# An attention and gated feed-forward layer on one core: the last group's scores two heads abreast

## The chip, the cores and the metric

The kernel runs on one core of a Trainium2 chip. The time is device microseconds of the whole program, the median of several runs. One further execution was taken by the profiler; its span is the time from its first to its last recorded work.

## What is computed

```python
xn = layernorm(x)                        # x: 1 x 1024 x 512, float32
q, k, v = xn @ wq + bq, xn @ wk + bk, xn @ wv + bv
# 32 query heads, 8 key/value heads, width 16; rope on q and k
s = softmax(q k^T / 4) v                 # 4 query heads share one key head
z = xn @ W^T + b
m = sum over 8 experts of ((xn @ A_e) @ B_e) * p_e      # rank 16 each
gamma = min(0.5 * |z| / (|m| + 1e-6), 1)                # by token
out = x + s * silu(z + gamma * m)
```

## The kernel before

A prelude loads and normalises x (eight tiles of 128 tokens), transposes it, projects q, k, v, turns q and k by rope and stacks them over partitions in three parts of 16 rows (a high part, used twice, and a low part), so that one pass in a single-pass float format gives the product at higher precision. Even groups lie in rows 0 to 47, odd ones in rows 64 to 111 (`ROWS = 64`); two more rows hold the negated row maxima in `qA` and ones in `kA`, so that a score matmul subtracts the maximum as well. The gate of the first four token tiles is also computed in the prelude.

Then come eight groups, one for each key head with its four query heads. A group has two halves of 512 queries, a half has eight tiles of 128 keys (tile s is 0 to 15 over both), a tile four heads: 64 scores of 128 keys x 512 queries. The work of a group is spread over the engines:

- TensorE writes a score into one of three banks of `st` (L970) and, in groups 0 to 6, behind each a row of scores of the next group with queries on the partitions (L863, in four banks of `sm`). After each burst of 3 scores (`BURST`) it runs one block of values (L924): `oT` sums probabilities x values, four heads in four column strips. Blocks are cut over columns (`CUTS`): 11 for a half, two bursts behind the scores (`LAG`). A half's sum is copied out by ScalarE (L561) and turned back to tokens by TensorE (L934).
- ScalarE takes each score through the exponential into `probs` (L596), which holds four key tiles (`PB`); it also copies the transposed maxima (L580 for half 1) and has the tanh of the gates (L528).
- VectorE reduces each row of scores to its maximum (L672); GpSimd splits the maxima in two parts, TensorE transposes them (L877), ScalarE copies them, and SyncE's queue sends them into the rows of `qA` (`maxima_row`, L298).

The last group (`LAST`, group 7) has no next group, so L863 is absent. In the free banks of `sm` it computes the dense part of the last four token tiles instead: five units for a tile t = 4 to 7, four matmuls of z (L943) and one of m (L946), put behind the bursts that `LATE_UNITS` names. VectorE adds the bias, copies m and squares both for the norms (`late_dense`: L757, L759, L764), GpSimd works out gamma (L392 to L401), VectorE sums (`gate_sum`, L686), ScalarE takes the tanh (L528), VectorE multiplies (`gate`, L692), and GpSimd multiplies and adds the first 448 columns (`add_late`, L480, L482), which SyncE stores (L337). The last 64 columns wait for the group's heads: copy (L561), turn (L934), reciprocal and scaling (L722, L725), gate and add on VectorE (L783, L785), store (L339). Each engine works through its own list in the order written, and waits on semaphores; SyncE's transfers are issued in order too.

Of the kernel before, what the change touches and what calls it, by code (L numbers as in the profile page):

```python
# [134 lines left out]
def sm_out0(g):  # L135
# [6 lines left out]
SM_LAST = {what: sm_base(LAST) + 2 * i for i, what in enumerate((4, "out1", 5, 6, 7, "out0", "tail"))}  # L142


LATE_UNITS = {2: [(4, 0), (4, 1)], 5: [(4, 2), (4, 3)], 8: [(4, NE)], 11: [(5, 0)], 14: [(5, 1), (5, 2)],
              17: [(5, 3), (5, NE)], 20: [(6, 0), (6, 1)], 23: [(6, 2), (6, 3)], 26: [(6, NE), (7, 0)],
              29: [(7, 1), (7, 2)], 31: [(7, 3)], 34: [(7, NE)]}


def build(nc, x, wq, wk, wv, biases, bv, wT, b, A, B, p_sc, cosT, sinT, ident, identb, ones, out):  # L150
    ctx = ExitStack()
    with ctx:
# [76 lines left out]

        def pj(n):  # L230
            return oT[:, :] if n % 4 == 3 else st[:, n % 4, :]
# [24 lines left out]
        late_copied, late_scaled, late_added = sem("late_copied"), sem("late_scaled"), sem("late_added")  # L256
# [25 lines left out]
        def _(sp):  # L282
# [18 lines left out]

            sp.wait_ge(ones_set, 1)
# [194 lines left out]
        def _(act):  # L497
# [58 lines left out]
            def evacuate(g, half, n, free):  # L556

                act.wait_ge(pv_done, blocks_through(g, NT * half + NT - 1))
                if free is not None:
                    act.wait_ge(sm_full, free)  # L560
                act.activation(heads[:, half, :], oT[:, :], ACT.Copy).then_inc(heads_out, 1)  # L561
# [7 lines left out]
            def step(g, first=False, last=False):  # L569
                for s in range(16):  # L570
                    for h in range(REP):
                        if 4 * s + h == OUT1_AT and not first and not last:
                            copy_turned(2 * g - 1, sm_out1(g))
                        if 4 * s + h == OUT0_AT and not last:
# [7 lines left out]
                        if 4 * s + h == MAX0_AT and not last:  # L582
# [4 lines left out]
                        late = 1 if last and 4 * s + h >= MAX0_AT else 0  # L587
                        act.wait_ge(st_full, st_score(g, s, h) + 1 - late)
# [7 lines left out]
                        act.activation(probs[:, s % PB, h, :], st[:, (st_score(0, s, h) - late) % 3, :], ACT.Exp,  # L596
                                       scale=float(D) ** -0.5).then_inc(st_free, 1)
                        if first and (s, h) in ((1, 3), (3, 3)):
                            gate_tanh_of({1: 2, 3: 3}[s])
                        if last and (s, h) in ((3, 3), (7, 3), (10, 3), (15, 3)):  # L600
                            gate_tanh_of({3: 4, 7: 5, 10: 6, 15: 7}[s])
                        if (s, h) == (1, 1) and not first:
                            evacuate(g - 1, 1, 2 * g - 1, sm_out1(g - 1) + 1)
                        if (s, h) == (9, 1):
                            evacuate(g, 0, 2 * g, None if first else sm_out0(g - 1) + 1)
# [4 lines left out]
            step(LAST, last=True)  # L610
            evacuate(LAST, 1, 2 * LAST + 1, SM_LAST["out1"] + 2)


        @block.vector
        def _(dve):
# [99 lines left out]
            def scale_heads(at, banks, n, to, done):  # L715

                bank = sm[:, at % 4, :].rearrange("p (t h c) -> p t h c", t=TH, h=REP)
                dve.wait_ge(sm_full, at + banks)
# [10 lines left out]
                dve.sem_inc(sm_free, banks)  # L729

            def hold_heads(g, at, banks):

                scale_heads(at, banks, 2 * g + 1, late_heads[:, :, g * (REP * D):(g + 1) * (REP * D)], None)
# [18 lines left out]
            def late_dense(t):  # L752

                n = SM_LAST[t]
                unread = uT[:, 0:HALF]
                dve.wait_ge(sm_full, n + 2)
                dve.tensor_tensor(dense(t), sm[:, n % 4, :], b_sb[:, :], ALU.add).then_inc(late_copied, 1)  # L757
                dve.wait_ge(gate_done, t - 2)
                dve.tensor_copy(m_sb[:, t % 3, :], sm[:, n % 4 + 1, :]).then_inc(late_copied, 1)  # L759
                dve.wait_ge(late_copied, 2 * (t - TH) + 2)  # L760
                dve.sem_inc(sm_free, 2)
# [6 lines left out]
            hold_heads(LAST - 1, SM_LAST["out1"], 2)  # L768
# [12 lines left out]
            scale_heads(SM_LAST["tail"], 2, 2 * LAST + 1, scaled[:, :, :], LAST + 1)  # L781
# [8 lines left out]
        def _(pe):  # L790
# [118 lines left out]
            def values(g, half, b):  # L909

                s = NT * half + block_parts(b)[-1][0]
                fewer = 1 if g == LAST and 4 * s + 3 >= MAX0_AT else 0
                pe.wait_ge(st_free, st_score(g, s, 3) + 1 - fewer)
# [15 lines left out]
            def turn_heads(half, at, banks, n_heads):  # L929

                pe.wait_ge(heads_out, n_heads)
                pe.wait_ge(sm_free, at + banks - 4)
                for t in range(TH):
                    mm = pe.transpose(sm[:, at % 4, t * P:(t + 1) * P], heads[:, half, t * P:(t + 1) * P], id_sb[:, :])  # L934
                mm.then_inc(sm_full, banks)

            def late_unit(t, c):

                n = SM_LAST[t]
                if c == 0:  # L940
                    pe.wait_ge(sm_free, n - 2)
                if c < NE:
                    pe.matmul(sm[:, n % 4, :], xT[:, 1, c, (t - TH) * P:(t - TH + 1) * P], wT_sb[:, c, :],  # L943
                              start=(c == 0), stop=(c == NE - 1))
                else:
                    pe.matmul(sm[:, n % 4 + 1, :], uT[:, t * P:(t + 1) * P], B_sb[:, :],  # L946
                              start=True, stop=True).then_inc(sm_full, 2)

            def group(g, first=False, last=False):
                rows = slice(ROWS * (g % 2), ROWS * (g % 2) + KM)  # L950
                for i in range(64):
# [6 lines left out]
                    if i == MAX0_AT and not last:  # L958
# [5 lines left out]
                    fewer = 1 if last and i >= MAX0_AT else 0  # L964
                    n = st_score(g, s, h) - fewer
# [6 lines left out]
                    if i == OUT1_AT + 3 and not first and not last:  # L972
                        pe.wait_ge(turned_out, 2 * g)
                    if i == OUT0_AT + 3 and not last:
                        pe.wait_ge(turned_out, 2 * g + 1)
                    if not last:
                        score_rows(g + 1, i, sm_score(g, i), 2 if first and i == OUT1_AT - 1 else 1)
# [8 lines left out]
                    if i == OUT1_AT - 1 and not first:  # L986
                        turn_heads(1, SM_LAST["out1"] if last else sm_out1(g), 2 if last else 1, 2 * g)
                    if i == OUT0_AT - 1:
                        turn_heads(0, SM_LAST["out0"] if last else sm_out0(g), 2 if last else 1, 2 * g + 1)
                    if last:  # L990
                        for unit in LATE_UNITS.get(i, ()):
                            late_unit(*unit)
# [64 lines left out]
```

## Time and profile before

| what | us |
|---|---|
| median of 3 runs (455.23 to 455.76) | 455.65 |
| the profiled execution | 455.27 |
| its span | 453.5 |
| TensorE matmul busy | 439.9 |
| VectorE busy | 370.8 |
| ScalarE busy | 308.1 |
| GpSimd busy | 134.4 |

Busy times are those of the profiled execution. Names of engines in the rows: PE is TensorE (PEld its weight loads), DVE VectorE, ACT ScalarE, POOL GpSimd, SPq SyncE's issues of transfers. L596 is line 596 of the kernel. Float32 matmuls are listed as two instructions each.

### The profile page before, as it was taken

The page shows a single profiled execution, that of the slowest core. Times are in us where ns is not written, and L with a number is a line of the kernel's source. Part 1 is how long each engine was busy: PE and PEld are TensorE (multiplying, and loading weights), DVE is VectorE, ACT ScalarE, POOL GpSimd, SP SyncE. Part 2 cuts the span into 40 slices and gives each one's busy share as a digit, 9 for nine tenths or more (in the row PEclk, how much of TensorE's full clock was granted, in tenths as well). Part 3 has the DMA queues.
Part 4 walks back from the last instruction along what each step waited for, and adds up shares of the span by engine and source line. Part 5 has one row for each costly group of instructions (what it writes and reads, how often), then busy time and mean ns, then how long its engine had stood idle before and what let it go on. Part 6 is the DMA issues. An engine that isn't in the chain of part 4 may idle for free.

```text
span 453.5 us, 8417 instructions
## 1 busy us (share of the span) xinstructions
PE 439.9 (97%) x3237; PEld 195.6 (43%) x3237; DVE 370.8 (82%) x613; ACT 308.1 (68%) x606; POOL 134.4 (30%) x185
## 2 busy tenths in 40 slices
PE   8897999999999999999999999999999999999995
PEld 3474443443344444444444444444444444433342
DVE  5662688888999999999999999999999999434522
ACT  2121011224889898898989889898988989654594
POOL 7573111434104030330403133040313304014451
PEclk9999799999899999999999999999999999999998
DMA  8989944444000000000000000000000000020011
GB/s 260 319 120 127 119 69 69 69 73 70 2 1 3 1 4 1 1 4 1 4 1 1 3 2 4 1 3 0 3 4 1 3 0 3 2 83 22 19 34 33
DMA packets 13368, 17.49 MB, mean 39 GB/s; under 512 B 3088, under 2 KB 7440, under 8 KB 13328
## 3 DMA queue, kind: packets, MB, share of 16 engines
q1 hardware_dynamic: 11808, 15.84, 18.7%
q10 hardware_dynamic: 1520, 1.12, 0.9%
q8 instruction: 25, 0.41, 0.4%
q14 instruction: 15, 0.12, 0.1%
HBM read 6.72 MB, written 2.10 MB: 19 GB/s over the span
## 4 chain that ended last, share of the span: by engine, by line
PE 86%; SPq 5%; DMA 4%; DVE 2%; issue 1%; ACT 1%; POOL 0%; DVEq 0%
PE st L970 35%; PE oT L924 30%; PE sm L863 7%; PE st L803 6%; PE sm L943 3%; SPq L316 2%; DMA kA<-arena 2%; PE sm L934 2%; DMA idb_sb<-in_identb 2%; PE oT L803 2%; DVE negmax L664 1%; PE sm L946 1%; SPq L284 1%; SPq L290 1%; PE st L892 0%
## 5 line engine op out<-in xcount | busy, mean ns | idle before, releaser
L596 ACT ACTIVATE arena<-st 128x512 f32<-128x512 f32 x512 | 267.0, 600 | 39.5 <-PE st L970 35.3
L672 DVE TENSOR_REDUCE neghalf<-sm 128x1 f32<-128x512 f32 x448 | 270.5, 678 | 4.6 <-PE sm L863 4.6
L863 PE MATMUL sm<-kA,qA 48*128 48x512 f32 x512 | 181.7, 448 | 3.7 <-DMA kA<-arena 3.4
L970 PE MATMUL st<-qA,kA 50*128 50x512 f32 x512 | 177.9, 444 | 1.1 <-ACT arena L596 1.0
L924 PE MATMUL oT<-arena,vg 128*32 128x256 f32 (+3 forms) x1792 | 147.3, 421 | 0.0
L970 PEld LDWEIGHTS st<-qA,kA 50*128 50x128 f32 x512 | 83.5, 185 | 113.6 <-ACT arena L596 92.1
L863 PEld LDWEIGHTS sm<-kA,qA 48*128 48x128 f32 x512 | 84.8, 186 | 21.1 <-issue 12.5
L443 POOL TENSOR_TENSOR rsum<-junk,consts 128x16 f32<-128x16 f32 x13 | 37.9, 2912 | 86.3 <-ACT junk L567 86.3
L924 PEld LDWEIGHTS oT<-arena,vg 128*32 128x32 f32 x1792 | 38.4, 108 | 53.6 <-issue 45.2
L664 DVE TENSOR_REDUCE negmax<-sm 128x1 f32<-128x1024 f32 x32 | 38.1, 1220 | 15.9 <-PE sm L863 15.6
L513 ACT ACTIVATE arena<-arena 128x512 fp32r<-128x512 f32 x10 | 6.3, 631 | 57.9 <-POOL arena L372 57.9
L412 POOL TENSOR_TENSOR maxp<-negmax,consts 128x16 bf16<-128x16 f32 x16 | 3.4, 213 | 120.8 <-DVE negmax L679 120.8
L372 POOL TENSOR_TENSOR arena<-arena 128x512 f32<-128x512 f32 x10 | 12.7, 1269 | 41.6 <-DVE arena L647 41.6
L757 DVE TENSOR_TENSOR xT_sb<-sm,b_sb 128x512 f32<-128x512 f32 x4 | 2.8, 692 | 17.4 <-PE sm L946 17.4
L803 PE MATMUL oT<-xT_sb,arena 128*128 128x512 f32 x32 | 16.9, 666 | 0.0
L943 PE MATMUL sm<-wT_sb,xT_sb 128*128 128x512 f32 x32 | 16.2, 619 | 0.0
L392 POOL TENSOR_TENSOR gam<-norms,consts 128x2 f32<-128x2 f32 x8 | 6.1, 761 | 32.7 <-DVE uT L764 23.4
L803 PE MATMUL st<-xT_sb,arena 128*128 128x512 f32 x32 | 15.5, 612 | 0.0
L376 POOL TENSOR_TENSOR arena<-arena 128x512 fp32r<-128x512 f32 x10 | 13.3, 1327 | 7.4 <-ACT arena L513 7.4
L803 PE MATMUL st<-wT_sb,xT_sb 128*128 128x512 f32 x32 | 15.5, 605 | 0.0
L561 ACT ACTIVATE wkv<-oT 128x512 f32<-128x512 f32 x16 | 9.6, 597 | 3.9 <-PE oT L924 3.9
L505 ACT ACTIVATE xT_sb<-st 128x512 f32<-128x512 f32 x7 | 4.0, 596 | 11.9 <-PE st L815 11.9
(94 smaller groups left out, 270.0 us busy)
## 6 DMA issues: line engine op xcount, KB each, us to landing
qA<-arena SPq DMA_DIRECT2D x48, 128.0 KB, 5.0
x_sb<-in_x SPq DMA_DIRECT2D x8, 256.0 KB, 6.0
kA<-arena SPq DMA_DIRECT2D x12, 128.0 KB, 6.7
wT_sb<-in_wT SPq DMA_DIRECT2D x1, 1024.0 KB, 9.3
out<-x_sb SPq DMA_DIRECT2D x1, 896.0 KB, 4.0
out<-x_sb SPq DMA_DIRECT2D x4, 224.0 KB, 2.0
z_sb<-in_wq SPq DMA_DIRECT2D x1, 768.0 KB, 10.3
wkv<-in_wk ACTq DMA_DIRECT2D x1, 256.0 KB, 4.4
```

Of the source, the lines that this page charges most:

```text
L372: pool.tensor_tensor(rot[:, n % 2, :], rot[:, n % 2, :], swp[:, n % 2, :], ALU.add).then_inc(rotated, 1)
L376: pool.tensor_tensor(parts[:, n % PART_BUFS, 1, :].bitcast(F32R), rot[:, n % 2, :], parts[:, n % PART_BUFS, 0, :], ALU.subtract).then_inc( ...
L443: pool.tensor_tensor(sums, came[:, :, :, D], consts[:, 2:3].unsqueeze(2).broadcast_to((P, TH, REP)), ALU.pow).then_inc(sums_inv, 1)
L561: act.activation(heads[:, half, :], oT[:, :], ACT.Copy).then_inc(heads_out, 1)
L596: act.activation(probs[:, s % PB, h, :], st[:, (st_score(0, s, h) - late) % 3, :], ACT.Exp, scale=float(D) ** -0.5).then_inc(st_free, 1)
L664: dve.tensor_reduce(negmax[:, e // 16, e % 16:e % 16 + 1], sm[:, n % 4:n % 4 + 2, :].rearrange("p a n -> p (a n)"), AX.X, ALU.max, negate= ...
L672: dve.tensor_reduce(neghalf[:, e // 16, e % 16, j % 2:j % 2 + 1], sm[:, n % 4, :], AX.X, ALU.max, negate=True).then_inc(sm_free, count)
L803: mm = pe.matmul(pj(n), weight[:, c, columns], moving[:, c, :], start=(c == 0), stop=(c == NE - 1))
L863: pe.matmul(sm[:, n % 4, :], qA[rows, half, g // 2, h, qt * P:(qt + 1) * P], kA[rows, g // 2, kh * HALF:(kh + 1) * HALF], start=True, stop ...
L924: mm = pe.matmul(oT[h * VC:(h + 1) * VC, cols], vg[:, g % 2, kt, :], probs[:, (NT * half + kt) % PB, h, cols], start=(kt == 0), stop=(kt = ...
L943: pe.matmul(sm[:, n % 4, :], xT[:, 1, c, (t - TH) * P:(t - TH + 1) * P], wT_sb[:, c, :], start=(c == 0), stop=(c == NE - 1))
L970: pe.matmul(st[:, n % 3, :], kA[rows, g // 2, kt * P:(kt + 1) * P], qA[rows, half, g // 2, h, :], start=True, stop=True).then_inc(st_full, 1)
```

## The change

The last group leaves the common loops of TensorE, ScalarE and SyncE and has its own. In group 1 three transfers copy the last group's keys, and its queries of heads 2 and 3, from rows 64 and up to rows 0 and up, over group 0's, which are read by then; four small ones put the maxima beside them. A tile's four scores are issued at once, in the order 0, 2, 1, 3, heads 0 and 1 from the upper rows, 2 and 3 from the lower, into a ring of four banks (three of `st`, one of `sm`). Values run over two whole key tiles in a block. The late units are issued up to three in a row, z into banks 3 and 0 of `sm`, m and the turned heads into bank 1. The maxima of the second half go through the ring ahead of tile 2 (before: ahead of the tenth score). The tanh of tiles 4, 5, 6 comes after key tiles 7, 10, 13 (before: 3, 7, 10), that of tile 7 behind the last copy of heads (before: ahead of it). The core of the diff:

```diff
-SM_LAST = {what: sm_base(LAST) + 2 * i for i, what in enumerate((4, "out1", 5, 6, 7, "out0", "tail"))}
-LATE_UNITS = {2: [(4, 0), (4, 1)], 5: [(4, 2), (4, 3)], 8: [(4, NE)], 11: [(5, 0)], 14: [(5, 1), (5, 2)],
-              17: [(5, 3), (5, NE)], 20: [(6, 0), (6, 1)], 23: [(6, 2), (6, 3)], 26: [(6, NE), (7, 0)],
-              29: [(7, 1), (7, 2)], 31: [(7, 3)], 34: [(7, NE)]}
+PAIRED = (0, 2, 1, 3)
+LAST_RING, LAST_MAX1 = 4, 8
+BANK_C, BANK_Z, BANK_M = 2, (3, 0), 1
+LAST_BANK_M = (4, "out1", 5, 6, "out0", 7, "tail")
+LATE_UNITS = {0: [(4, 0), (4, 1), (4, 2)], 1: [(4, 3), (4, NE), (5, 0)], 2: [(5, 1), (5, 2), (5, 3)],
+              3: [(5, NE), (6, 0), (6, 1)], 4: [(6, 2), (6, 3), (6, NE)], 5: [(7, 0), (7, 1), (7, 2)],
+              6: [(7, 3), (7, NE)]}
+def last_score(s, k):
+    i = 4 * s + k
+    return i + (i >= LAST_MAX1)
+def last_values(s):
+    return 2 * BLOCKS * LAST + (s // 2 + 1 if s < 2 * NT - 2 else s - NT + 2)
...
+            def low_maxima(half):
+                for part in range(2):
+                    sp.dma_start(qA[KR + part:KR + part + 1, half, 0, 2:4, :].bitcast(F32)
+                                 .rearrange("p h (r c) -> p (h r) c", c=P),
+                                 maxT[16 * part + 8:16 * part + 16, half, :].bitcast(F32)).then_inc(low_max, 16)
+            def low_rows():
+                for n in range(len(halves)):
+                    sp.wait_ge(stacked[n], 16 * SLOT_DMAS)
+                for half in range(2):
+                    sp.dma_start(qA[0:KR, half, 0, 2:4, :].bitcast(F32),
+                                 qA[ROWS:ROWS + KR, half, LAST // 2, 2:4, :].bitcast(F32)).then_inc(low_in, 16)
+                sp.dma_start(kA[0:KR, 0, :].bitcast(F32),
+                             kA[ROWS:ROWS + KR, LAST // 2, :].bitcast(F32)).then_inc(low_in, 16)
...
-            for g in range(KV):
+            for g in range(LAST):
                 sp.wait_ge(st_free, st_max1(g) + 1)
                 sp.wait_ge(max_in, 16 * (2 * g + 1))
                 maxima_row(g, 1)
-                if g < LAST:
-                    sp.wait_ge(st_free, st_max0(g) + 1)
-                    sp.wait_ge(max_in, 16 * (2 * g + 2))
-                    maxima_row(g + 1, 0)
+                if g == 1:
+                    low_rows()
+                sp.wait_ge(st_free, st_max0(g) + 1)
+                sp.wait_ge(max_in, 16 * (2 * g + 2))
+                maxima_row(g + 1, 0)
+            low_maxima(0)
+            sp.wait_ge(last_free, LAST_MAX1 + 1)
+            sp.wait_ge(max_in, 16 * (2 * LAST + 1))
+            maxima_row(LAST, 1)
+            low_maxima(1)
...
-                        if last and (s, h) in ((3, 3), (7, 3), (10, 3), (15, 3)):
-                            gate_tanh_of({3: 4, 7: 5, 10: 6, 15: 7}[s])
...
-            step(LAST, last=True)
-            evacuate(LAST, 1, 2 * LAST + 1, SM_LAST["out1"] + 2)
+            for s in range(2 * NT):
+                if 4 * s == LAST_MAX1:
+                    act.wait_ge(last_full, LAST_MAX1 + 1)
+                    act.wait_ge(max_in, 16 * 2 * LAST)
+                    act.activation(maxT[:, 1, :], last_bank(LAST_MAX1).bitcast(BF16)[0:32, 0:P],
+                                   ACT.Copy).then_inc(last_free, 1)
+                act.wait_ge(pv_done, last_values(s - PB) if s >= PB else blocks_through(LAST - 1, s - PB + 2 * NT))
+                for k, h in enumerate(PAIRED):
+                    act.wait_ge(last_full, last_score(s, k) + 1)
+                    act.activation(probs[:, s % PB, h, :], last_bank(last_score(s, k)), ACT.Exp,
+                                   scale=float(D) ** -0.5).then_inc(last_free, 1)
+                if s == 1:
+                    evacuate(2 * BLOCKS * LAST, 1, (sm_full, sm_out1(LAST - 1) + 1))
+                if s == NT + 1:
+                    evacuate(last_values(NT - 1), 0, (sm_full, sm_out0(LAST - 1) + 1))
+                if s in (7, 10, 13):
+                    gate_tanh_of({7: 4, 10: 5, 13: 6}[s])
+            evacuate(last_values(2 * NT - 1), 1, (m_full, LAST_BANK_M.index("out1") + 1))
+            gate_tanh_of(7)
...
-            hold_heads(LAST - 1, SM_LAST["out1"], 2)
+            scale_heads("out1", 2 * LAST - 1, late_heads[:, :, LATE - REP * D:LATE], None)
             gate_sum(4)
             late_dense(5)
             gate(4)
             late_dense(6)
             gate(5)
             gate_sum(6)
+            scale_heads("out0", 2 * LAST, scaled[:, :, :], LAST)
             late_dense(7)
-            scale_heads(SM_LAST["out0"], 2, 2 * LAST, scaled[:, :, :], LAST)
             gate(6)
             gate_sum(7)
             gate(7)
-            scale_heads(SM_LAST["tail"], 2, 2 * LAST + 1, scaled[:, :, :], LAST + 1)
+            scale_heads("tail", 2 * LAST + 1, scaled[:, :, :], LAST + 1)
...
+            def last_scores(s):
+                half, kt = s // NT, s % NT
+                if kt == 0:
+                    pe.wait_ge(max_in, 16 * (2 * LAST + half + 1))
+                    pe.wait_ge(low_max, 32 * (half + 1))
+                for k, h in enumerate(PAIRED):
+                    n = last_score(s, k)
+                    rows, place = (slice(ROWS, ROWS + KM), LAST // 2) if h < 2 else (slice(0, KM), 0)
+                    claim_last(n)
+                    pe.matmul(last_bank(n), kA[rows, place, kt * P:(kt + 1) * P], qA[rows, half, place, h, :],
+                              start=True, stop=True).then_inc(last_full, 1)
+            def claim_last(n):
+                if n >= LAST_RING:
+                    pe.wait_ge(last_free, n - LAST_RING + 1)
+                elif n == 3:
+                    pe.wait_ge(sm_free, sm_score(LAST - 1, 60) + 1)
+                else:
+                    pe.wait_ge(st_free, st_score(LAST - 1, 15, n + 1) + 1)
+            def last_block(*tiles):
+                pe.wait_ge(last_free, last_score(tiles[-1], 3) + 1)
+                if tiles[0] % NT == 0:
+                    pe.wait_ge(heads_out, 2 * LAST + tiles[0] // NT)
+                for s in tiles:
+                    for h in range(REP):
+                        mm = pe.matmul(oT[h * VC:(h + 1) * VC, :], vg[:, LAST % 2, s % NT, :], probs[:, s % PB, h, :],
+                                       start=(s % NT == 0), stop=(s % NT == NT - 1))
+                mm.then_inc(pv_done, 1)
...
+            def last_group():
+                pe.wait_ge(low_in, 48)
+                pe.wait_ge(v_ready, LAST + 1)
+                for u in range(NT):
+                    if 8 * u == LAST_MAX1:
+                        pe.wait_ge(max_parts, 2 * LAST + 2)
+                        claim_last(LAST_MAX1)
+                        turn_maxima(last_bank(LAST_MAX1), 1).then_inc(last_full, 1)
+                    last_scores(2 * u)
+                    if u == 0:
+                        values(LAST - 1, 1, BLOCKS - 2)
+                    if u == NT - 1:
+                        last_block(2 * u - 2, 2 * u - 1)
+                    for unit in LATE_UNITS.get(u, ()):
+                        late_unit(*unit)
+                    if u == 5:
+                        last_turn("out0", 0, 2 * LAST + 1)
+                    last_scores(2 * u + 1)
+                    if u == 0:
+                        values(LAST - 1, 1, BLOCKS - 1)
+                    elif u < NT - 1:
+                        last_block(2 * u - 2, 2 * u - 1)
+                    if u == 1:
+                        last_turn("out1", 1, 2 * LAST)
+                last_block(2 * NT - 2)
+                last_block(2 * NT - 1)
+                last_turn("tail", 1, 2 * LAST + 2)
             group(0, first=True)
             for n in range(len(halves) - 2, len(halves)):
                 pe.wait_ge(stacked[n], 16 * SLOT_DMAS)
             for g in range(1, LAST):
                 group(g)
-            group(LAST, last=True)
-            for b in range(BLOCKS - LAG, BLOCKS):
-                values(LAST, 1, b)
-            turn_heads(1, SM_LAST["tail"], 2, 2 * LAST + 2)
+            last_group()
```

## Rows read from the trace of the kernel before

**Rows 1.** The page's slices: 40 equal parts of the span, in tenths.
```profile
PE   8897999999999999999999999999999999999995
...
PEclk9999799999899999999999999999999999999998
```

**Rows 2.** Chain of waits, the last group: share of its time by line.
```profile
by line: PE st L970 33.5%; PE oT L924 31.4%; PE sm L943 26.2%; PE sm L946 6.9%; PE sm L934 2.0%; PE st L877 0.3%; issue 0.0%
```

**Rows 3.** Windows, the same stretch: busy us (instructions) by engine, clock, DMA.
```profile
389.10:447.60 58.50, 58.45 (x357) 23.04 (x353) 19.99 (x39) 36.85 (x72) 18.34 (x31) 1.00 0.09 31
```

**Rows 4.** Chain of waits in order of time: start us, us, what.
```profile
417.58 0.57 PE oT L924 x8
418.15 1.05 PE sm L946 x2
...
420.07 0.90 PE st L970 x3
...
421.75 1.91 PE sm L943 x4
423.67 0.66 PE st L970 x2
...
429.57 1.00 PE oT L924 x8
```

**Rows 5.** Timeline of TensorE in group 0: start us, us, instruction.
```profile
131.24 0.50 PE L970 MATMUL st<-qA,kA 50*128 50x512 f32 x1
131.24 0.49 PE L863 MATMUL sm<-kA,qA 48*128 48x512 f32 x1
131.57 0.39 PE L970 MATMUL st<-qA,kA 50*128 50x512 f32 x1
...
131.90 0.86 PE L924 MATMUL oT<-arena,vg 128*32 128x128 f32 x16
```

**Rows 6.** The page's DMA issues: count, KB each, us to landing.
```profile
qA<-arena SPq DMA_DIRECT2D x48, 128.0 KB, 5.0
```

**Rows 7.** Timeline at the start of the last group.
```profile
389.06 0.96 PE L970 MATMUL st<-qA,kA 50*128 50x512 f32 x3
...
389.60 1.58 ACT L596 ACTIVATE arena<-st 128x512 f32<-128x512 f32 x3 [0.37 <-PE st L970]
...
394.46 0.60 ACT L561 ACTIVATE wkv<-oT 128x512 f32<-128x512 f32 x1
...
399.45 0.27 ACT L580 ACTIVATE maxT<-st 32x128 fp32r<-32x128 bf16 x1 [1.10 <-PE st L877]
```

**Rows 8.** Timeline of the end.
```profile
446.24 0.63 ACT L528 ACTIVATE m_sb<-xT_sb 128x512 f32<-128x512 f32 x1
...
446.91 0.69 DVE L692 SCALAR_TENSOR_TENSOR xT_sb<-m_sb,xT_sb 128x512 f32<-128x512 f32 x1 [4.12 <-ACT m_sb L528]
447.62 0.60 ACT L561 ACTIVATE wkv<-oT 128x512 f32<-128x512 f32 x1 [0.74 <-PE oT L924]
447.68 1.14 POOL L480 TENSOR_TENSOR late_heads<-late_heads,xT_sb 128x448 f32<-128x448 f32 x1 [5.68 <-DVE xT_sb L692]
...
448.96 0.26 DVE L722 RECIPROCAL rsum<-sm 128x16 f32<-128x16 f32 x1 [1.36 <-PE sm L934]
...
450.05 0.33 SPq L337 DMA_DIRECT2D out<-x_sb  x1
...
450.79 0.38 SPq L339 DMA_DIRECT2D out<-x_sb  x1
```

**Rows 9.** Timeline around the gamma of the last late tile.
```profile
439.70 0.72 POOL L392 TENSOR_TENSOR gam<-norms,consts 128x2 f32<-128x2 f32 x1
...
442.03 0.75 DVE L686 SCALAR_TENSOR_TENSOR xT_sb<-m_sb,gam,xT_sb 128x512 f32<-128x512 f32 x1 [5.21 <-POOL gam L401]
```

**Rows 10.** Windows in group 0: busy us of PE, PEld, DVE, ACT, POOL; granted clock.
```profile
110.00:115.00 5.00, 4.14 (x17) 1.42 (x15) 5.00 (x9) 3.10 (x8) 2.25 (x7) 1.00 0.14 15
115.00:120.00 5.00, 5.00 (x29) 1.71 (x27) 5.00 (x9) 4.31 (x10) 0.46 (x3) 0.66 0.01 3
```

More of the change, by code:

```diff
@@ L554, in _, with evacuate @@
             squares(3)
-            def evacuate(g, half, n, free):
-                act.wait_ge(pv_done, blocks_through(g, NT * half + NT - 1))
+            def evacuate(blocks, half, free):
+                act.wait_ge(pv_done, blocks)
                 if free is not None:
-                    act.wait_ge(sm_full, free)
+                    act.wait_ge(*free)
                 act.activation(heads[:, half, :], oT[:, :], ACT.Copy).then_inc(heads_out, 1)
@@ L581, in step @@
                                            ACT.Copy).then_inc(st_free, 1)
-                        if 4 * s + h == MAX0_AT and not last:
+                        if 4 * s + h == MAX0_AT:
                             act.wait_ge(st_full, st_max0(g) + 1)
@@ L586, in step @@
                                            ACT.Copy).then_inc(st_free, 1)
-                        late = 1 if last and 4 * s + h >= MAX0_AT else 0
-                        act.wait_ge(st_full, st_score(g, s, h) + 1 - late)
+                        act.wait_ge(st_full, st_score(g, s, h) + 1)
                         if h == 0 and not (first and s < PB):
@@ L713, in _, with scale_heads @@
                     dve.tensor_tensor(z_sb[:, i, :], pj(e), b_sb[:, :], ALU.add).then_inc(pj_dve, 1)
-            def scale_heads(at, banks, n, to, done):
-                bank = sm[:, at % 4, :].rearrange("p (t h c) -> p t h c", t=TH, h=REP)
-                dve.wait_ge(sm_full, at + banks)
+            def scale_heads(what, n, to, done):
+                use = LAST_BANK_M.index(what)
+                bank = sm[:, BANK_M, :].rearrange("p (t h c) -> p t h c", t=TH, h=REP)
+                dve.wait_ge(m_full, use + 1)
                 dve.wait_ge(heads_scaled, n)
@@ L911, in values @@
                 s = NT * half + block_parts(b)[-1][0]
[L912 to L913 removed]
+                pe.wait_ge(st_free, st_score(g, s, 3) + 1)
                 if b == 0:
@@ L927, in values, with turn_heads, group @@
                 mm.then_inc(pv_done, 1)
-            def turn_heads(half, at, banks, n_heads):
+            def turn_heads(half, bank, n_heads):
                 pe.wait_ge(heads_out, n_heads)
-                pe.wait_ge(sm_free, at + banks - 4)
                 for t in range(TH):
[L934 to L949, printed above, removed]
+                    mm = pe.transpose(bank[:, t * P:(t + 1) * P], heads[:, half, t * P:(t + 1) * P], id_sb[:, :])
+                return mm
+            def group(g, first=False):
                 rows = slice(ROWS * (g % 2), ROWS * (g % 2) + KM)
@@ L957, in group @@
                         turn_maxima(st[:, st_max1(0) % 3, :], 1).then_inc(st_full, 1)
-                    if i == MAX0_AT and not last:
+                    if i == MAX0_AT:
                         pe.wait_ge(max_parts, 2 * g + 3)
@@ L963, in group @@
                         pe.wait_ge(max_in, 16 * (2 * g + half + 1))
-                    fewer = 1 if last and i >= MAX0_AT else 0
-                    n = st_score(g, s, h) - fewer
+                    n = st_score(g, s, h)
                     if first and i < 3:
@@ new lines, in claim_m, with last_turn, late_unit @@
+            def claim_m(what):
+                use = LAST_BANK_M.index(what)
+                if use == 0:
+                    pe.wait_ge(sm_free, sm_score(LAST - 1, 63) + 1)
+                else:
+                    pe.wait_ge(m_free, use)
+            def last_turn(what, half, n_heads):
+                claim_m(what)
+                turn_heads(half, sm[:, BANK_M, :], n_heads).then_inc(m_full, 1)
+            def late_unit(t, c):
+                if c < NE:
+                    if c == 0 and t < TH + 2:
+                        pe.wait_ge(sm_free, sm_score(LAST - 1, 62) + 1)
+                    elif c == 0:
+                        pe.wait_ge(z_free, t - TH - 1)
+                    mm = pe.matmul(sm[:, BANK_Z[t % 2], :], xT[:, 1, c, (t - TH) * P:(t - TH + 1) * P], wT_sb[:, c, :],
+                                   start=(c == 0), stop=(c == NE - 1))
+                    if c == NE - 1:
+                        mm.then_inc(z_full, 1)
+                else:
+                    claim_m(t)
+                    pe.matmul(sm[:, BANK_M, :], uT[:, t * P:(t + 1) * P], B_sb[:, :],
+                              start=True, stop=True).then_inc(m_full, 1)
```

52 lines of the change are left out of this document (27 added, 25 removed).

## The prediction, made before the change was run

> **What bounds the kernel now.** I read the page's slices first [rows 1]: TensorE is busy in nine tenths or more of nearly every slice, at full granted clock, so its work is the first suspect everywhere; what it shares its time with has to be read stage by stage. The diff leaves groups 0 to 6 alone but for transfers, so I cut the trace at the last group. Between its first score at 389.06 and the last copy of heads at 447.62 the chain of waits is TensorE alone [rows 2], and the window of the same stretch says the same from the other side: TensorE 58.45 us busy of 58.50, ScalarE 36.85, VectorE 19.99, GpSimd 18.34 [rows 3]. So in this stage a us taken from TensorE is a us gained, until another engine is met; from rows 3 that could be ScalarE, 21 us below.
>
> The shares of rows 2 split the 58.5 us: scores L970 19.6, values L924 18.4, late tiles' matmuls L943 and L946 19.4, two turns of heads L934 1.2, the turn of the maxima 0.2. Then I looked at what one piece costs in the chain [rows 4]. Three scores in a row take 0.90, two take 0.66: so 0.23 for one more, and 0.43 for the last with the change to the next kind. A block of values takes 1.00 for 512 columns and 0.57 for 256: 0.43 per 256 columns and 0.145 for the change of kind. Late units (one 512-column matmul, which the chain lists as two) take 1.05 for one and 1.91 for two: 0.86 each and 0.19 for the change. These prices give the group back: scores 20 x 0.90 + 2 x 0.66 = 19.3; values 16 key tiles x 0.855 + 22 blocks x 0.145 = 16.9, with the two blocks of group 6 (0.57 + 1.00) 18.4; late 20 x 0.86 + 12 batches x 0.19 = 19.5; turns 1.4. Sum 58.6, measured 58.6.
>
> **The change part by part.**
>
> Scores abreast. In the groups before, a score of group g and a score row of g+1 use the two halves of TensorE's rows. The timeline shows what that costs [rows 5]: at 131.24 both start within 0.01, at 131.57 both again, and the values start at 131.90. Two pairs take 0.66, what two single scores take. The last group has no next group to pair with, so it pays 0.66 for two scores; with heads 0 and 2, then 1 and 3, on different rows it should pay 0.66 for four. Price 16 tiles x 0.66 = 10.6 for 19.3: 8.7 less. That both matmuls of a pair wait for the same engine and write neighbouring banks is new; I keep it for the rivals.
>
> Values. 7 blocks of two key tiles and 2 single ones instead of 22: 13 changes of kind fewer, 13 x 0.145 = 1.9. Late units: 7 batches instead of 12: 5 x 0.19 = 1.0. The two turns stay. TensorE's work from 389.06 becomes 58.6 - 8.7 - 1.9 - 1.0 = 47.0.
>
> Copied rows and their maxima. Three transfers of 48 rows x 4 KB in group 1, four small ones for the maxima. The nearest transfers take 5.0 us to land [rows 6]. They wait in SyncE's queue behind the first maxima row of group 1 and ahead of the next one, which SyncE sends only half a group later; they are used in the last group. The maxima's copies for half 0 are sent when ScalarE has copied group 6's maxima, 23 exponentials before the last group, at 0.49 each (below) 11 us ahead; for half 1 about 18 us ahead (below). Cost nothing; if the cover were gone, at most the 5 us of a landing, once.
>
> Now the waits, since all four heads of a tile must have their banks. ScalarE: three exponentials take 1.58, one such pass 0.60, so 0.49 from start to start; the first starts 0.54 after its score (389.06 to 389.60) [rows 7]. Four are over 0.54 + 3 x 0.49 + 0.60 = 2.61 after the tile's first score. A full round of the new order is scores 0.66, three units 2.77, scores 0.66, block of two tiles 1.85: 5.94. After the first scores TensorE is away 2.77: the banks are all free. After the second it is away 1.85, back 2.51 after they began; the first pair needs the first two banks (free at 1.63), the second pair, 0.33 later at 2.84, needs the last (2.61). No wait, by 0.2.
>
> I walk the rounds. Round 0: scores 389.06 to 389.72, block of group 6 0.57, units 2.77, scores 393.06 to 393.72, block of group 6 1.00: 394.72. Round 1 holds the one stall: the maxima are turned into the ring's bank (0.13, to 394.85), and the fourth score of tile 2 needs that bank back. ScalarE runs tile 1's exponentials from 393.60 (last starts 395.07), then the copy of heads, which this order puts before the maxima copy (0.50), then the maxima copy (0.27 [rows 7]): free at 396.35. So the fourth score starts at 396.4, not at 395.2: 1.2 lost. The row maxima go to SyncE only then, and are needed in round 4, 18 us later. Rounds 1 to 3 end at 402.65 (with a turn 0.59), 408.6, 414.5; in round 4 the tanh of tile 4 stands before tile 8's exponentials, 0.3 more at most, 420.4; round 5 with the other turn 426.9; round 6 has two units, 5.08: 432.0. Round 7 has none: scores 432.0 to 432.65, block 434.5, scores 435.15, the single block of tile 14 to 436.15. Then the block of tile 15 waits for the last exponential: first one at 435.03, last one over at 437.1. A second exposed wait, 1.0. Block to 438.2. That is 389.06 + 47.0 + 1.2 + 1.0 = 438.2, against 447.6 before: 9.4 earlier.
>
> The end does not follow by 9.4. Before, the last late tile was gated (446.91) ahead of the last copy of heads (447.62) [rows 8]. Now its tanh stands behind the copy of heads (438.25 to 438.85) and the chain to it is long. The tanh of tile 6 follows tile 13's exponentials: 432.0 to 432.6, its gate on VectorE 0.69 to 433.35; GpSimd then adds tile 6 (2.37, as 447.68 to 450.05 [rows 8]) to 435.7, works out gamma of tile 7 (439.70 to 442.03, 2.33 [rows 9]) to 438.05, VectorE sums (0.75) to 438.8. Both inputs of the tanh come within 0.1 of each other at 438.8; tanh 0.63 [rows 8] to 439.45; gate 0.69 to 440.2. The last heads, turned at 439.6 (1.34 from the copy's start, 447.62 to 448.96), wait 0.6 behind that gate; VectorE ends 1.83 later (448.96 to 450.79) at 442.05. GpSimd's add of tile 7 runs 440.2 to 442.6, its store is issued at 442.65, and the last store behind it in SyncE's queue at 443.05 (0.4 for an issue). Before, the last store was issued at 450.79 and the span ended 2.7 later at 453.5. So the end goes from 453.5 to 445.75: 7.75 less. The late tile, not the heads, now sets the end; 1.65 of the 9.4 is given back there.
>
> The profiled execution took 455.27, 1.77 around its span. 455.27 - 7.75 = 447.5; the median of the runs is 0.38 above that execution: 447.9.
>
> A rule that speaks against the change is weighed here. Rows 3 leave ScalarE 21 us below TensorE, and the walk finds it in the way only twice. The Trainium skill (TensorEngine Tiling (Array Packing), PSUM Bottleneck) says that tiling speeds up TensorE but not the emptying of its banks, which may become the limit. By rows the sum stays as it stands; by that rule the second rival comes out.
>
> **The rivals.**
>
> The clock falls. In group 0, TensorE was idle for 0.86 of the 5 us from 110 among spaced scores, and in the next 5 us its granted clock averaged 0.66 [rows 10]: with levels of 1.2 and 2.4 GHz, 3.4 us at the lower one. The new round 1 has a wait of 1.2 among scores and a small turn, the end one of 1.0. Against it: these stand among dense blocks of values and late units, and the same trace kept the full clock through all of the last group. 3.4 us at half clock lose 1.7: 449.6, two such stretches 451.3.
>
> ScalarE late at every tile. The margin was 0.2 at the second pair. If the first pair too had to wait for all four banks, TensorE, back at 2.51, would stand until 2.61, 0.1 in each of seven rounds, 0.7: 448.6; if 0.1 is lost at each of the 16 tiles, 1.6: 449.5. This is where that rule would lead.
>
> The two heads don't run abreast, but one behind the other at 0.23: a tile costs 3 x 0.23 + 0.43 = 1.12, 0.46 more, 16 tiles 7.4: 455.3, no change. Against it stand rows 5 and the like in every burst of seven groups.
>
> Slower than before: each change of rows drains the array, 0.43 a score, 1.72 a tile: 1.06 x 16 = 17 more, 465. It decides against the change from 1.15 a tile (7.75 / 16 above 0.66). For it speaks only that the pairing within one tensor and on one engine's releases isn't in the trace.
>
> Better than forecast: no stall at the maxima, and the late chain shorter: 446.2.
>
> **How the numbers follow.** Forecast 0.60 (own range 446.9 to 449.0); clock 0.15; ScalarE late at every tile 0.12; better 0.04; one behind the other 0.04; drained, or a transfer in the way, 0.05. The range reaches from 446.2 to 451.2, which leaves out the last two cases and part of the others. 0.2% is 0.9 us, about what a measurement of this kernel tells from no change. Faster 0.91, within 0.04, slower 0.05.
>
> **What the profile would show.** Two scores starting within 0.01 in pairs, four in 0.66; L924 and the late units at 15 + 1.6 and 18.6; the fourth score of tile 2 released by ScalarE's maxima copy 1.2 late; a gap of 1.0 before the last block; evacuation near 438.2, the last gate after it, and the tile-7 store last but one at 442.6. The prediction is wrong if the pairs stand apart, if the clock's digits fall in the last group, or if ScalarE releases scores in most tiles.

## The result, and the profile after

The changed kernel takes 451.23 us (median of 4 runs, 450.94 to 452.56), the kernel before 455.44 (4 runs, 454.24 to 455.76): ratio 0.9912, 95% interval 0.9886 to 0.9938. It is faster by 4.2 us, not by the 7.75 forecast, and lies just outside the range (451.2). The profiled execution took 451.26 with a span of 449.5, against 455.27 and 453.5.

From one execution to another the last group begins at times up to 5 us apart, whatever is in it. So stretches are compared from one mark: the start of the block of values just ahead of the last group's first scores. Before it stands at 388.28, after at 388.13 (first row below); to the end of the span that is 65.2 before and 61.4 after, 3.85 less.

Windows of the changed kernel over its last group, which answer to [rows 3] (us, then busy us of PE, PEld, DVE, ACT, POOL, clock, DMA):

```profile
388.90:442.10 53.20, 49.91 (x261) 17.88 (x257) 17.91 (x38) 35.61 (x72) 17.76 (x31) 0.97 0.10 34
```

and its chain of waits by line over the same stretch, which answers to [rows 2]:

```profile
by line: PE sm L1085 30.7%; PE oT L1061 26.5%; PE st L1042 13.9%; PE sm L1091 6.8%; issue 6.2%; ACT arena L659 5.7%; PE sm L1042 5.2%; ACT wkv L604 2.3%; PE sm L987 1.9%; PE oT L978 1.9%; ACT maxT L654 0.2%; ACTq L658 0.0%
```

TensorE is no longer busy throughout (49.91 of 53.20), and the clock averages 0.97. The chain has an entry that wasn't there: "issue", time in which the profile names no releaser, 6.2% or 3.3 us. The timeline of TensorE says where most of it is:

```profile
388.13 0.86 PE L978 MATMUL oT<-arena,vg 128*32 128x128 f32 x16
391.11 0.70 PE L1042 MATMUL st<-qA,kA 50*128 50x512 f32 x3 [2.11 <-issue]
391.44 0.39 PE L1042 MATMUL sm<-qA,kA 50*128 50x512 f32 x1
391.77 0.86 PE L978 MATMUL oT<-arena,vg 128*32 128x256 f32 x8
392.56 4.27 PE L1085 MATMUL sm<-wT_sb,xT_sb 128*128 128x512 f32 x6
```

TensorE stands still for 2.11 us ahead of the last group's first score. Then three late units take 4.27, where three take 2.84 later on. Windows of 1 us tell why (the window's length, TensorE's busy us and instructions, then the granted clock):

```profile
390.00:391.00 1.00, 0.00 (x0) 1.00 0.00 0
391.00:392.00 1.00, 0.90 (x8) 1.00 0.00 0
392.00:393.00 1.00, 1.00 (x9) 0.53 0.00 0
393.00:394.00 1.00, 1.00 (x2) 0.50 0.00 0
394.00:395.00 1.00, 1.00 (x2) 0.50 0.00 0
395.00:396.00 1.00, 1.00 (x3) 0.77 0.00 0
```

About 1 us after the idle stretch the clock falls to its lower level, 1.2 GHz, for 3.4 us: 0.47 + 0.50 + 0.50 + 0.23 = 1.70 us of work lost. Gap and clock together are 3.8 us, the size of the miss in the stretch (7.75 forecast, 3.85 measured). The timeline of GpSimd over the idle time:

```profile
390.38 0.22 POOL L458 TENSOR_TENSOR maxp<-negmax,maxp 128x16 bf16<-128x16 f32 x1
390.55 0.45 POOL L466 TENSOR_TENSOR vg<-v_sb,bv_sb 128x128 f32<-128x128 f32 x1
```

The values of the last group (`vg`, L466) are ready at 391.00, and TensorE starts its weight load at 391.07. `last_group` begins with `pe.wait_ge(v_ready, LAST + 1)`; before, that wait stood ahead of the group's first block of values, behind nine of its scores. GpSimd makes `vg` only behind the maxima, and these wait for the last row of scores of group 6 on VectorE. So far this is argued: the profile itself names no releaser for the 2.11. The experiments test it.

### The profile page after: what moved, and what is told of

It reads as the page before. It is cut to its first block, busy times and chain, and to the rows that moved or that the text cites. A ratio compares the mean times of both kernels' runs of the same rounds, so it can differ in the third digit from the quotient of the medians.

```text
span 449.5 us, 8242 instructions
## 1 busy us (share of the span) xinstructions
PE 432.0 (96%) x3141; PEld 190.9 (42%) x3141; DVE 370.5 (82%) x613; ACT 307.3 (68%) x606; POOL 133.3 (30%) x185
## 3 DMA queue, kind: packets, MB, share of 16 engines
q10 hardware_dynamic: 1520, 1.12, 0.9%
## 4 chain that ended last, share of the span: by engine, by line
PE 85%; DMA 4%; SPq 3%; DVE 3%; ACT 2%; issue 2%; POOL 0%; DVEq 0%; ACTq 0%
PE st L1010 31%; PE oT L978 26%; PE sm L918 6%; PE st L858 6%; PE sm L1085 4%; PE oT L1061 3%; DMA kA<-arena 2%; PE sm L987 2%; DMA idb_sb<-in_identb 2%; PE st L1042 2%; PE oT L858 2%; DVE negmax L721 1%; PE st L894 1%; SPq L305 1%; PE sm L1091 1%
## 5 line engine op out<-in xcount | busy, mean ns | idle before, releaser
L638 ACT ACTIVATE arena<-st 128x512 f32<-128x512 f32 x448 | 233.3, 600 | 19.7 <-PE st L1010 15.8
L1010 PE MATMUL st<-qA,kA 50*128 50x512 f32 x448 | 156.6, 445 | 1.0 <-ACT arena L638 0.7
L978 PE MATMUL oT<-arena,vg 128*32 128x256 f32 (+3 forms) x1568 | 129.6, 422 | 0.0
L1010 PEld LDWEIGHTS st<-qA,kA 50*128 50x128 f32 x448 | 73.3, 185 | 97.5 <-ACT arena L638 84.4
L978 PEld LDWEIGHTS oT<-arena,vg 128*32 128x32 f32 x1568 | 33.5, 108 | 46.1 <-issue 38.2
L659 ACT ACTIVATE arena<-st 128x512 f32<-128x512 f32 x48 | 27.0, 602 | 16.4 <-PE st L1042 16.4
L1085 PE MATMUL sm<-wT_sb,xT_sb 128*128 128x512 f32 x32 | 17.1, 660 | 0.0
L1061 PE MATMUL oT<-arena,vg 128*32 128x512 f32 x128 | 15.6, 599 | 1.0 <-ACT arena L659 1.0
```

What stands on the lines that cost most here:

```text
L638: act.activation(probs[:, s % PB, h, :], st[:, st_score(0, s, h) % 3, :], ACT.Exp, scale=float(D) ** -0.5).then_inc(st_free, 1)
L659: act.activation(probs[:, s % PB, h, :], last_bank(last_score(s, k)), ACT.Exp, scale=float(D) ** -0.5).then_inc(last_free, 1)
L978: mm = pe.matmul(oT[h * VC:(h + 1) * VC, cols], vg[:, g % 2, kt, :], probs[:, (NT * half + kt) % PB, h, cols], start=(kt == 0), stop=(kt = ...
L1010: pe.matmul(st[:, n % 3, :], kA[rows, g // 2, kt * P:(kt + 1) * P], qA[rows, half, g // 2, h, :], start=True, stop=True).then_inc(st_full, 1)
L1061: mm = pe.matmul(oT[h * VC:(h + 1) * VC, :], vg[:, LAST % 2, s % NT, :], probs[:, s % PB, h, :], start=(s % NT == 0), stop=(s % NT == NT - 1))
L1085: mm = pe.matmul(sm[:, BANK_Z[t % 2], :], xT[:, 1, c, (t - TH) * P:(t - TH + 1) * P], wT_sb[:, c, :], start=(c == 0), stop=(c == NE - 1))
```

## The experiments

Each ratio is against runs of the kernel before on the same chip, with its 95% interval. Beside it stands the stretch from the mark to the span's end in the one profiled execution (before 65.2, changed kernel 61.4), which is free of what varies ahead of the last group.

**e1, the wait moved.**

```diff
             def last_block(*tiles):
...
+                if tiles[0] == 0:
+                    pe.wait_ge(v_ready, LAST + 1)
...
                 pe.wait_ge(low_in, 48)
-                pe.wait_ge(v_ready, LAST + 1)
```

> The changed kernel with the wait for the last group's values moved from ahead of its first score to ahead of its first block of values. Theory A (the wait for GpSimd's values keeps TensorE idle 2.1 us ahead of the first score, and the half clock from 392 to 395.5, 1.7 us, is what follows from that gap): both go, 451.2 - 2.1 - 1.7 = 447.4. Rival B (the clock falls because the start of the new last group is sparse anyway, its stall at the maxima included): the gap goes, the half clock stays or moves, 449.1. Rival C (the gap is the copied rows or the code, not the values): 451.2.

Measured 448.22 (5 runs), ratio 0.9836 (0.9810 to 0.9862), stretch 57.5: 3.9 less than the changed kernel, 7.7 less than before. Timeline of TensorE:

```profile
389.58 0.73 PE L1042 MATMUL st<-qA,kA 50*128 50x512 f32 x3
389.92 0.39 PE L1042 MATMUL sm<-qA,kA 50*128 50x512 f32 x1
390.24 0.64 PE L978 MATMUL oT<-arena,vg 128*32 128x256 f32 x8
390.81 2.84 PE L1087 MATMUL sm<-wT_sb,xT_sb 128*128 128x512 f32 x6
...
395.31 0.99 PE L1042 MATMUL st<-qA,kA 50*128 50x512 f32 x2
396.29 0.49 PE L1042 MATMUL sm<-qA,kA 50*128 50x512 f32 x1
396.89 0.49 PE L1042 MATMUL st<-qA,kA 50*128 50x512 f32 x1
```

The gap is gone and the units take 2.84. The granted clock reads 1.00 in every window of the group up to 440, and the wait at the maxima (395.31 to 396.89) is still there. It isn't an idle stretch, though: the scores come one by one, and the window from 396 to 397 has TensorE 0.89 busy. Theory A holds, rivals B and C don't.

**e2, the gap filled.** In the changed kernel, TensorE does two matmuls without use while it waits.

```diff
                 pe.wait_ge(low_in, 48)
+                pe.wait_ge(sm_free, sm_score(LAST - 1, 61) + 1)
+                for _ in range(2):
+                    pe.matmul(sm[:, BANK_Z[0], :], xT[:, 1, 0, 0:P], wT_sb[:, 0, :], start=True, stop=True)
                 pe.wait_ge(v_ready, LAST + 1)
```

> The changed kernel with two more 512-column float32 matmuls (0.86 us each, their result is overwritten) between the last values of group 6 and the wait for the last group's values, so that TensorE waits as long but stands idle for some 0.3 us only. Theory A: first score at the same time, full clock behind it, 451.2 - 1.7 = 449.5. Rival B (the clock doesn't hang on the gap): 451.2 with the half clock still there.

The timeline of TensorE now names the releaser:

```profile
390.23 1.98 PE L1099 MATMUL sm<-wT_sb,xT_sb 128*128 128x512 f32 x4
392.38 0.73 PE L1042 MATMUL st<-qA,kA 50*128 50x512 f32 x3 [0.16 <-POOL vg L466]
...
393.61 2.84 PE L1085 MATMUL sm<-wT_sb,xT_sb 128*128 128x512 f32 x6
```

The first score comes 2.93 after the mark (2.98 in the changed kernel), but the clock stays at 1.00 and the units take 2.84. The stretch is 59.65, 1.7 less than in the changed kernel: theory A in the trace. The timed runs don't show it: 451.0 (6 runs), ratio 0.9906 (0.9880 to 0.9932) beside 0.9912 (0.9886 to 0.9938) for the changed kernel, where theory A wanted 1.7 us less, about 0.9875. Taken alone they lean to rival B; two intervals of this width don't tell 1.7 us from none, and the spread of the runs (449.3 to 452.4) is wider than that.

**e5, the same wait in the kernel before.**

```diff
             def group(g, first=False, last=False):
+                if last:
+                    pe.wait_ge(v_ready, LAST + 1)
```

> The kernel before with one line more: TensorE waits for the last group's values ahead of that group's first score instead of ahead of its first block of values. Theory A (the wait costs 2.1 us by itself, in any order of the group, and a stretch at half clock follows from it): 2.1 to 3.8 more than before, with the same idle 2.1 ahead of the first score; the half clock costs up to 1.7. Rival (the order of the new last group is what makes the wait dear; before, other work would take it up): under 0.5 more.

Measured 459.6 (4 runs), ratio 1.0094 (1.0066 to 1.0123): slower by 4.3. Stretch 69.0, 3.8 more than before. Timeline of TensorE and 1 us windows:

```profile
391.30 0.96 PE L972 MATMUL st<-qA,kA 50*128 50x512 f32 x3 [2.06 <-POOL vg L423]
...
392.75 3.67 PE L943 MATMUL sm<-wT_sb,xT_sb 128*128 128x512 f32 x4
```

```profile
393.00:394.00 1.00, 1.00 (x2) 0.50 0.00 0
394.00:395.00 1.00, 1.00 (x2) 0.50 0.00 0
395.00:396.00 1.00, 1.00 (x2) 0.50 0.00 0
```

Here the profile does say it: 2.06 waiting for GpSimd's `vg`. The half clock follows, from 1.5 us after TensorE starts again, 1.71 us lost in all (windows 392 to 397: 0.88, 0.50, 0.50, 0.50, 0.91). The wait costs the same 3.8 in the old order of the group as in the new; nothing of the new order is needed for it. Here the timed runs say something too: the interval is 3.0 to 5.6 us slower, more than the gap of 2.06 alone.

**e3, no scores abreast.** On e1:

```diff
-                    rows, place = (slice(ROWS, ROWS + KM), LAST // 2) if h < 2 else (slice(0, KM), 0)
+                    rows, place = slice(ROWS, ROWS + KM), LAST // 2
```

> As e1_wait_moved, but all four heads' scores from the upper rows (the original place), so that none runs beside another. Theory A (a tile of four costs 0.66 us abreast and 3 x 0.23 + 0.43 = 1.12 one behind the other, and TensorE sets the pace): 16 x 0.46 = 7.4 more than e1_wait_moved, 454.8, with full clock. Rival (ScalarE sets the pace in the new order, so abreast or not matters little): under 2 us more than e1_wait_moved.

Measured 453.63 (10 runs), ratio 0.9967 (0.9944 to 0.9990); stretch 63.5, 6.0 more than e1. The ratios are 6.0 us apart as well. A burst of four takes 1.11 to 1.14 (the first 389.17 to 390.31) for 0.66, on average 1.12 as priced, 0.46 x 16 = 7.4. Of this 1.4 is absorbed, because two waits shrink when TensorE comes later: at the maxima the fourth score starts 1.16 behind the first, where it would start 0.82 behind it without a wait (1.58 and 0.34 in e1), 0.9 less waiting, and the last block waits 0.52 instead of 0.98. TensorE sets the pace; the rival with less than 2 us doesn't hold.

**e4, the maxima copy first.** On e1:

```diff
-                if s == 1:
+                if s == 2:
                     evacuate(2 * BLOCKS * LAST, 1, (sm_full, sm_out1(LAST - 1) + 1))
```

> As e1_wait_moved, but ScalarE's last copy of group 6's heads stands behind key tile 2's exponentials instead of behind tile 1's, so that the maxima copy that the fourth score of tile 2 waits for comes 0.5 us earlier. Theory A (TensorE's work sets the end of the group, a wait taken from it is taken from the whole): 0.5 less than e1_wait_moved, 446.9. Rival (the wait is only moved, to the first block of values, which now waits for that copy of heads): no difference.

Stretch 57.0, 0.5 less than e1. In the timeline tile 2's fourth score starts 7.6 after the mark instead of 8.1. Timed 447.93 (5 runs), ratio 0.9853 (0.9825 to 0.9882), which doesn't tell it from e1; 0.5 us is below what these runs resolve. That rests on one profiled execution of each.

**e8, gamma early; e7, tanh ahead; e6, both.** e8 and e7 on e1, e6 on e4:

```diff
             finish(LAST, 0, LAST, z_sb)
-            add_late(6)
             gamma(7)
+            add_late(6)
             add_late(7)
```

is e8's, and

```diff
-            evacuate(last_values(2 * NT - 1), 1, (m_full, LAST_BANK_M.index("out1") + 1))
             gate_tanh_of(7)
+            evacuate(last_values(2 * NT - 1), 1, (m_full, LAST_BANK_M.index("out1") + 1))
```

is e7's; e6 has both.

> As e1_wait_moved, but the last late tile's gamma ahead of the sixth tile's addition in GpSimd's list; the tanh stays behind the last copy of heads. Theory A (both inputs of the tanh, the gated sum and ScalarE behind the copy, come within 0.1 us of each other): taking only the one early gains nothing, within 0.2 of e1_wait_moved on the group's own time. Rival (GpSimd's chain alone sets the end): 1.4 earlier.

> As e1_wait_moved, but the last late tile's tanh ahead of the last copy of heads, as in the kernel before; GpSimd's order as changed. Theory A (the tanh's input comes at the same time as the copy's end, so the copy would wait for it): the last copy of heads is 1.0 later, the late tile's gate no earlier, the end within 0.5 of e1_wait_moved. Rival (the place of the tanh is what costs the 1.65 that the end lost): 1 us or more earlier than e1_wait_moved.

> As e4_maxima_first, but the last late tile's gamma ahead of the sixth tile's addition in GpSimd's list, and its tanh ahead of the last copy of heads on ScalarE, where ScalarE waits for TensorE anyway. Theory A (behind the last matmul the end hangs on the late tile's chain: gamma, sum, tanh, gate, addition, store): the late tile's store is out 2 us earlier, the heads set the end again with their 1.83 us on VectorE, and the end comes 1.4 us earlier than in e4_maxima_first. Rival (the end hangs on TensorE and the heads alone): the same as e4_maxima_first.

e8: 448.73 (4 runs), ratio 0.9849 (0.9817 to 0.9881), stretch 57.5, the same as e1. e7: 448.36 (4 runs), ratio 0.9847 (0.9818 to 0.9876), stretch 57.6, also the same; its copy of heads is 1.1 later. e6: 445.24 (6 runs), ratio 0.9788 (0.9758 to 0.9817), stretch 55.3, 1.7 less than e4 (the ratios are 3.0 us apart, give or take 1.9). The end of e1 by the timeline:

```profile
437.76 1.07 PE L1063 MATMUL oT<-arena,vg 128*32 128x512 f32 x8 [0.98 <-ACT arena L659]
...
438.66 0.75 DVE L743 SCALAR_TENSOR_TENSOR xT_sb<-m_sb,gam,xT_sb 128x512 f32<-128x512 f32 x1 [4.74 <-POOL gam L444]
438.90 0.60 ACT L604 ACTIVATE wkv<-oT 128x512 f32<-128x512 f32 x1 [1.19 <-PE oT L1063]
439.44 0.63 ACT L571 ACTIVATE m_sb<-xT_sb 128x512 f32<-128x512 f32 x1
...
440.11 0.69 DVE L749 SCALAR_TENSOR_TENSOR xT_sb<-m_sb,xT_sb 128x512 f32<-128x512 f32 x1 [0.70 <-ACT m_sb L571]
...
442.09 1.19 POOL L525 TENSOR_TENSOR x_sb<-x_sb,late_heads 128x448 f32<-128x448 f32 x1
442.32 1.23 DVE L840 TENSOR_TENSOR x_sb<-x_sb,xn 128x256 f32<-128x256 f32 x1
443.30 0.33 SPq L380 DMA_DIRECT2D out<-x_sb  x1
443.68 0.43 SPq L382 DMA_DIRECT2D out<-x_sb  x1
```

and of e6:

```profile
438.80 0.65 ACT L571 ACTIVATE m_sb<-xT_sb 128x512 f32<-128x512 f32 x1
...
439.48 0.69 DVE L749 SCALAR_TENSOR_TENSOR xT_sb<-m_sb,xT_sb 128x512 f32<-128x512 f32 x1 [1.33 <-ACT m_sb L571]
...
440.13 0.60 ACT L604 ACTIVATE wkv<-oT 128x512 f32<-128x512 f32 x1 [0.68 <-PE oT L1063]
...
442.62 0.33 SPq L380 DMA_DIRECT2D out<-x_sb  x1
...
443.36 0.38 SPq L382 DMA_DIRECT2D out<-x_sb  x1
```

In e1 the tanh's two inputs, the sum (438.66 + 0.75) and ScalarE behind the copy, come together at 439.4; moving one alone gains nothing, moving both 1.7 (the expectation had 1.4). From the copy of heads to the last store it is 4.8 us in e1 and 3.2 in e6, as in the kernel before [rows 8]. e6 is the fastest kernel of this study.

**e9, one key tile to a block; e10, the same on e6.** A block behind each tile's scores:

```diff
-    return 2 * BLOCKS * LAST + (s // 2 + 1 if s < 2 * NT - 2 else s - NT + 2)
+    return 2 * BLOCKS * LAST + s + 1
...
-                    if u == NT - 1:
-                        last_block(2 * u - 2, 2 * u - 1)
+                    else:
+                        last_block(2 * u - 2)
...
-                    elif u < NT - 1:
-                        last_block(2 * u - 2, 2 * u - 1)
+                    else:
+                        last_block(2 * u - 1)
```

> As e1_wait_moved, but with one key tile to a block of values behind each tile's scores. Theory A (a change of kind of work costs 0.145 us, seven more are paid; at the end the last scores start earlier and TensorE has a tile's values more to do while ScalarE works, so 0.5 of the 1.0 idle ahead of the last block is taken up): 0.5 more than e1_wait_moved. Rival (two tiles at a time is worth what the columns say, in waits too): 1.0 or more.

> e6_late_tile_early with one key tile to a block of values. Theory A: 0.5 more than e6_late_tile_early, since the late tile no longer sets the end. If the tail gain is larger than the changes of kind cost, less.

Neither came out as expected. e9 took 453.11 (10 runs), ratio 0.9948 (0.9925 to 0.9972), stretch 62.8: 5.3 more than e1 (5.1 by the ratios), not 0.5. Timeline of TensorE in one round:

```profile
406.80 1.06 PE L1063 MATMUL oT<-arena,vg 128*32 128x512 f32 x8
...
407.79 0.57 PE L1042 MATMUL st<-qA,kA 50*128 50x512 f32 x2
...
408.35 0.50 PE L1042 MATMUL sm<-qA,kA 50*128 50x512 f32 x1
...
408.84 0.50 PE L1042 MATMUL st<-qA,kA 50*128 50x512 f32 x1
```

Behind one tile's block TensorE is back at the scores 1.66 after the tile's first, and ScalarE needs 2.61 to empty the four banks. The scores come as the banks do, 0.5 apart and no longer abreast: 1.48 for a burst (407.79 to 409.27) instead of 0.66. That is 0.82 in each of six bursts, 4.9. I had counted the changes of kind and not the banks. e10 took 453.9 (12 runs), ratio 0.9960 (0.9932 to 0.9987), stretch 65.05, 9.8 more than e6 (7.8 by the ratios). There the first block needs the copy of heads already behind tile 2's scores, and ScalarE has that copy behind tile 2's exponentials (397.73 to 398.33); TensorE stands idle for 1.95 up to 398.42. The granted clock falls too, and already within that idle stretch:

```profile
397.00:398.00 1.00, 0.00 (x0) 0.82 0.08 21
398.00:399.00 1.00, 0.58 (x4) 0.50 0.05 15
```

It stays at 0.50 until 404.4, so the 6.0 us from 398.42 on lose 3.0. With 2.0 for the gap and 4.9 for the bursts, which are as in e9, that makes 9.9; the stretch has 9.8.

## Why the prediction was wrong, step by step

**The step that failed** is the first line of the walk, "Round 0: scores 389.06 to 389.72". The last group's first score also waits for `v_ready`, which the change moved ahead of it from behind the ninth. The prediction named the waits for banks and row copies and didn't list this one; GpSimd's `vg` comes at 391.00, so it costs 2.1 (e1, e5). The wait stands in the diff, and the trace of the kernel before has the row:

```profile
390.69 0.45 POOL L423 TENSOR_TENSOR vg<-v_sb,bv_sb 128x128 f32<-128x128 f32 x1
```

`vg` is ready at 391.14 there, 2.1 after that group's first score at 389.06 [rows 7], and TensorE asks for it only behind nine scores, at 397.13. That the measured 451.23 lies only just above the range is chance: the top of the range, 451.2, answers to two stretches at half clock, and what came was one such stretch and a wait that wasn't in the sum.

**The clock** was a rival at 0.15, priced at 1.7 a stretch, and one such stretch came, worth 1.70. It came from that gap, not from the places the rival named: with the gap gone both stay, the wait of 1.2 at the maxima and the one of 1.0 at the end, and the clock of the group reads 1.00 (e1). The prediction counted falling digits of the clock as a sign that it is wrong; the page's 40 slices are too long for that, they all read 9 over the last group of the changed kernel, and only the windows of 1 us show the fall. The timed runs show gap and clock together: ratio 0.9836 without them and 0.9912 with them, 3.5 us, and 4.3 in e5, whose interval leaves out a gap alone. The split of 2.1 and 1.7 rests on profiled executions, one of each kernel: the three with an idle stretch of about 2 us in the group show the half clock (changed kernel, e5, e10), the others don't.

**All else came out as worked out.** Without the gap the stretch shrinks by 7.71 (e1); forecast 7.75.
- Scores abreast: four in 0.66, partners starting within 0.01 of each other, as in [rows 5]. That they share a releasing engine and a ring of banks doesn't matter while the banks are free; it does when they aren't (e9). Worth 6.0 (e3) where the sum had 8.7: of the 8.7, 1.4 comes from bursts of four instead of three (16 x 1.12 = 17.9 for 19.3), without anything abreast, and 1.4 of the other 7.4 turns into waits, which the walk counted separately.
- Values: in the changed kernel a block of two tiles takes 1.85 (416.42 to 418.27), and three units take 2.77, as priced. But two tiles at a time do more than save 13 changes of kind: they fill the time in which ScalarE empties the ring. The term of 1.9 was right for the change; taken alone, putting one tile behind each burst costs 5.3.
- The wait at the maxima: fourth score 1.58 behind the first (395.31 to 396.89 in e1), walk 1.55. The wait ahead of the last block: 0.98, walk 1.0. Copies of rows: group 1 runs as before, TensorE without a gap from 140 to 200.
- The end: the late tile's store at 443.30 and the last one 0.38 behind it (e1), as walked, 0.1 later than the walk has it when both are counted from the first score. The chain through gamma and tanh gives back what the walk said (1.65; e6 returns 1.7).
- The second rival, where the Trainium skill's rule would lead (TensorEngine Tiling (Array Packing), PSUM Bottleneck), isn't borne out by the changed kernel: at the second burst of each full round no score waits. e9 shows its mechanism: there the emptying does limit the bursts, and the trace agrees with the rule.

## What to carry to other kernels

When a stage gets a loop of its own, list every wait of its engines before and after with the time at which each is satisfied; a wait moved up from behind nine scores to ahead of the first cost half the gain here. A gap on TensorE may have to be paid twice, once as idle time and once as clock. A burst that fills a whole ring needs as much other work between bursts as the ring takes to empty; where two inputs of one step tie, moving one shows nothing, so try both together.

## What the runs showed of the hardware

- After TensorE stood idle for 2.1 us among otherwise dense work, its granted clock was at the lower of its two levels for some 3.4 us, beginning 1 to 1.5 us after it started again (changed kernel, e5). In e10, where the idle stretch was 1.95, the clock fell within the stretch, 1.2 after its start, and stayed low for 6.8. The idle 1.0 at the end of e1 and the 1.2 by which its fourth score came late at the maxima had no such effect. The prediction had the fall as a rival from a row of group 0 [rows 10]. So the stretch cost nearly twice its own length in the changed kernel and e5 (3.8), and 5.0 in e10.
- VectorE's last addition (L840) takes 1.23 us in e1 and 0.42 in e6 and before. In e1 it starts at 442.32 beside GpSimd's L525 (442.09 to 443.28) and ends at 443.55, 0.27 after it; the product ahead of it, L838, ends at 442.29, 0.28 after GpSimd's L523 (442.01). In e6 the sum L743 takes 1.62 (e1: 0.75) beside GpSimd's L523 (436.46 to 437.61) and ends at 438.16. L783, which reads a bank of PSUM, takes its usual 0.42 beside GpSimd's L523. So in these rows VectorE's instructions on two tiles in SBUF end only after GpSimd's does. In e1 it costs nothing: the last store stands in SyncE's queue behind the late tile's store in any case.
